# Gated delta rule beside an FP4 feed-forward layer: a loop that overlaps steps of three elements, a second buffer of values, and lanes that GpSimd turns

## The chip, the cores and the metric

One core of a Trainium2 chip runs the whole program. The metric is device time in microseconds (us): the median of the executions shown, and beside it one execution that the hardware profiler took. The engines are TensorE (PE, matrix products and transposes, out of SBUF into PSUM), VectorE (DVE), ScalarE (ACT), GpSimd (POOL) and SyncE (SP, which here only starts DMA transfers). Each has its own instruction stream, in order, and they meet at semaphores.

## What is computed

Input is x of shape (32, 256, 128): 32 independent elements of a batch, 256 steps of time, 128 channels, float32. For each element, with xn the layer norm of x:

```python
q = silu(causal_conv(xn @ Wq)); k = silu(causal_conv(xn @ Wk)); v = silu(causal_conv(xn @ Wv))
gk = -exp(A_log) * softplus(xn @ Wgk + dt_bias); beta = sigmoid(xn @ Wb + b_b)
q = l2norm(q) * 64 ** -0.5; k = l2norm(k)          # 12 heads, 64 wide; v: 12 heads, 128 wide
def step(S, (qt, kt, vt, bt, gt)):                 # 256 steps of time, S: 64 x 128 for each head
    S = S * exp(gt)
    delta = (vt - kt @ S) * bt
    S = S + outer(kt, delta)
    return S, qt @ S
o = scan(step); o = o * rsqrt(mean(o * o) + 1e-5) * g_norm_weight
attn = (o * silu(xn @ Wg)) @ Wo
ffn = fp4_linear(silu(fp4_linear(xn, w_gate)) * fp4_linear(xn, w_up), w_down)   # 352 hidden
out = x + attn + ffn
```

fp4_linear rounds both operands to an FP4 grid with one scale for each 16 numbers.

## The kernel before, in words

The scan over time is done in two chunks of 128 steps. Inside a chunk the recurrence becomes a triangular system for each head, 2 x 12 = 24 units for an element. `UP` holds for each unit the 128x128 triangle and the decayed products of queries and keys. The triangle is inverted in three stages. First its four diagonal 32x32 blocks are inverted on POOL: the blocks of all units are brought by DMA to one partition each (96 "lanes", tile `laneA`), where each lane is solved column by column with two instructions a column, 30 columns in all (`LANEP`). The columns grow from 30 numbers to 240 and shrink again. `LOUT` writes the blocks to DRAM (4 transfers), `LLOAD` reads them as lanes, `STORE` writes the solved lanes, `FETCH` puts them back into `UP` (4 transfers). Then PE joins 32-blocks to 64-blocks (`MY`, `MZ`) and those to 128 (`MY2`, `MX`, `MZ2`). For `MY` one operand must be turned: `MT` on DVE transposes solved blocks 0 to 2 of `UP` into `N64` (three instructions for each third of the units).

One element is cut into some 200 named steps, and the table `ORDER` at the head of the file is the program: each engine walks it and issues its own part of each step, in that order. A step is (kind, number, offset): in iteration `it` it works on element `it + offset`. With offset 1 stands the front of the next element: `LN`, `LN2` (layer norm), `XN` (transpose on PE), `ZB` (gates; `ZBr`, `ZBe`, `ZBg` read them), `QK`, `QKr`, `QKt`, `QKs` (keys and queries: product on PE, first tap on ACT, three taps of the convolution on DVE, silu on ACT), `QT`, `QN` (squares and their sums), `CJ` (scales), `DDg`, `DD` (decays: POOL, PE, ACT), `GR`, `GRr` (products of keys, scaled into `UP` by DVE), `VP`, `VPt`, `VPs` (values), `XQ`, `FU`, `HQ`, `HT` (feed-forward), `VT` (values turned into `V`), `KT`, and three of the four `LANEP` pieces. With offset 0 stands the back of the current element: the last piece, `STORE`, `FETCH`, `MT` to `MZ2`, then the recurrence in slots 3 to 18 (`SE` on PE and ACT, `SO` on PE and DVE, `SQ` squares on ACT), `OS` (POOL takes a power -0.5), `GP` (output gates), `OG` (DVE multiplies), `OT`, `WO` (output product), `YO`, `YOr`. The 12 heads pass through the slots as through a pipe, one head a slot.

Six PSUM banks (`ring`) are handed out along the table by `ring_plan`. Keys, queries, `UP` and several small tiles exist twice, taken by the parity of the element (`par()`); `V` exists once, so that `VT` of the next element waits for `OT` of the current one. Iterations -1 and 0 are written out, then a hardware loop runs two iterations a round, then the last is written out. In the profile L873 to L876 are `LN`, L880 `LN2` (its power -0.5 is POOL L538), L885 `ZBr`, L899 a part of `ZBg`, L856 the taps, L950 `GRr`, L1005, L1007 and L1011 `SO`, L1016 the DVE part of `OS` and L577 its POOL part, L1027 `OG`, L1034 `YOr`, L986 `MT`, L563, L568 and L571 `LANEP`, L549 `DDg`, L1098 `XN`, L1324 `WO`.

The lines that join layer norm to POOL's queue, and the turning that DVE does:

```python
if kind == "LN":                     # GpSimd
    pool.wait_ge(s_var, cnt(i, 1, 1))
    nc.gpsimd.tensor_tensor(out=rstd[:, :], in0=veps[:, :], in1=mhalf[:, 0:NT],
                            op=ALU.pow).then_inc(s_rstd, 1)
```

Of the kernel before, what the change touches and what calls it, by code (L numbers as in the profile page):

```python
# [23 lines left out]
PIECES = 4  # L24
# [27 lines left out]
    ("VT", 2, 0), ("LN", 0, 1), ("LN2", 0, 1), ("VT", 5, 0), ("VTr", 2, 0), ("XN", 0, 1), ("XNr", 0, 1),  # L52
    ("QK", 0, 1), ("ZB", 0, 1), ("ZBr", 0, 1), ("QK", 1, 1), ("QKr", 0, 1), ("ZBe", 0, 1), ("QK", 2, 1),
    ("QKt", 0, 1), ("QKr", 1, 1), ("ZBg", 0, 1), ("LANEP", 3, 0), ("DDg", 0, 1), ("STORE", 0, 0), ("QKs", 0, 1),
    ("QK", 3, 1), ("VT", 4, 0), ("QKr", 2, 1), ("VP", 0, 1), ("QKt", 1, 1), ("QKs", 1, 1), ("QKt", 2, 1),
    ("QKr", 3, 1), ("VTr", 5, 0), ("VTr", 4, 0), ("DD", 0, 1), ("FETCH", 0, 0), ("VPr", 0, 1), ("QKs", 2, 1),
    ("QT", 0, 1), ("QTr", 0, 1), ("QKt", 3, 1), ("MT", 0, 0), ("QN", 0, 1), ("QT", 1, 1), ("QTr", 1, 1),
    ("MT", 1, 0), ("QT", 2, 1), ("DDg", 1, 1), ("DD", 1, 1), ("QTr", 2, 1), ("QKs", 3, 1), ("DDr", 0, 1),
    ("GC", 0, 1), ("MY", 0, 0), ("DDg", 2, 1), ("MYr", 0, 0), ("XQ0", 0, 1), ("QN", 1, 1), ("VP", 1, 1),
    ("GCr", 0, 1), ("QK", 4, 1), ("MZ", 0, 0), ("DDr", 1, 1), ("DD", 2, 1), ("QKr", 4, 1), ("MZr", 0, 0),  # L60
    ("DDg", 3, 1), ("DDr", 2, 1), ("MY2", 0, 0), ("MY", 1, 0), ("QKt", 4, 1), ("QT", 3, 1), ("VP", 2, 1),
    ("MYr", 1, 0), ("VPr", 1, 1), ("MY2r", 0, 0), ("VPr", 2, 1), ("QTr", 3, 1), ("MZ", 1, 0), ("MT", 2, 0),
    ("SSr", 0, 1), ("MY", 2, 0), ("MZr", 1, 0), ("DD", 3, 1), ("MYr", 2, 0), ("DDr", 3, 1), ("QN", 2, 1),
    ("MX", 1, 0), ("MZ2r", 0, 0), ("CJ", 0, 1), ("QK", 5, 1), ("SE", 3, 0), ("VPt", 1, 1), ("MY2r", 1, 0),
    ("QKs", 4, 1), ("MZ", 2, 0), ("GR", 0, 1), ("VPt", 2, 1), ("VPt", 0, 1), ("GRr", 0, 1), ("GRr", 1, 1),
    ("QKr", 5, 1), ("DDg", 4, 1), ("SE", 4, 0), ("MZr", 2, 0), ("GR", 1, 1), ("QKt", 5, 1), ("XQ0", 1, 1),
# [1287 lines left out]
```

## Time and profile before

| what | value |
|---|---|
| median of 3 executions | 3294.02 us (3276.98 to 3296.87) |
| profiled execution, own time | 3276.51 us |
| its span from first to last instruction | 3274.8 us |
| busy, share of the span | PE 83%, PEld 65%, DVE 80%, ACT 67%, POOL 47% |
| mean granted clock of PE | 0.937 |
| DMA engines, mean busy share | 0.1 (22 GB/s) |

Busy time is the union of an engine's instructions. No engine is busy all the time, so the question for each stretch is which wait ends last there. The profiled execution lies 17.5 us under the median; sums below are made against its span of 3274.8 us.

### The profile page before, as it was taken

To read this page: it belongs to the slowest core of one execution; us is meant where nothing else is said; L and a number is where in the kernel's file an instruction comes from. 1 tells how busy PE (TensorE), PEld (TensorE's weight loads), DVE (VectorE), ACT (ScalarE), POOL (GpSimd) and SP (SyncE) were. 2 spreads that over 40 slices of the span, in tenths; PEclk is the share of its full clock that TensorE was granted. 3 is DMA by queue.
4 is the path that set the end of the run, shared out by engine and by line. 5 is a ranking of instruction groups with operands and counts; after the bars stand their busy time and mean duration, and the time that the engine had idled before them with its cause. 6 is when DMAs were issued, how large, how long until landed. Compare 5 with 4: busy or idle time off the path is not lost.

```text
span 3274.8 us, 84555 instructions
## 1 busy us (share of the span) xinstructions
PE 2721.0 (83%) x25330; PEld 2140.6 (65%) x25487; DVE 2617.8 (80%) x7460; ACT 2193.7 (67%) x6594; POOL 1549.4 (47%) x2386
## 2 busy tenths in 40 slices
...
GB/s 48 22 25 18 20 27 14 27 26 17 23 26 16 26 22 17 26 18 23 26 20 19 27 15 26 26 17 23 26 16 26 26 16 23 27 15 27 26 15 14
DMA packets 241563, 73.30 MB, mean 22 GB/s; under 512 B 207408, under 2 KB 234352, under 8 KB 241008
## 3 DMA queue, kind: packets, MB, share of 16 engines
...
## 4 chain that ended last, share of the span: by engine, by line
DVE 33%; POOL 27%; issue 23%; DMA 6%; PE 6%; SPq 2%; POOLq 1%; DVEq 1%; ACT 1%; ACTq 0%
POOL laneA L571 12%; POOL laneT L568 12%; DVE KQ L856 8%; DVE UP L950 8%; DVE vc L856 4%; DVE N L986 3%; DMA laneA<-to_lanes 3%; DMA to_lanes<-UP 3%; PE ring L1127 2%; POOL rO L577 2%; SPq L473 1%; POOLq L533 1%; DVE ssr L919 1%; DVE xn L880 1%; DVE V L1005 1%
## 5 line engine op out<-in xcount | busy, mean ns | idle before, releaser
L571 POOL TENSOR_TENSOR laneA<-laneA,laneT 96x30 f32<-96x30 f32 (+14 forms) x960 | 514.7, 536 | 75.6
L568 POOL TENSOR_TENSOR laneT<-laneA 96x30 f32<-96x30 f32 (+14 forms) x960 | 488.4, 509 | 68.1 <-POOL laneA L571 0.2
L555 POOL TENSOR_TENSOR sqk<-sse,phalf 128x8 f32<-128x8 f32 x96 | 157.3, 1638 | 700.5 <-DVE sse L924 700.5
L856 DVE SCALAR_TENSOR_TENSOR KQ<-ring,ckq,KQ 128x255 f32<-128x255 f32 (+2 forms) x1152 | 462.9, 475 | 14.4 <-DVE nabs L888 7.0
L856 DVE SCALAR_TENSOR_TENSOR vc<-ring,cvv,vc 128x255 f32<-128x255 f32 (+2 forms) x1152 | 460.0, 475 | 1.2
L549 POOL TENSOR_TENSOR gm<-g,mle 128x512 f32<-128x512 f32 x192 | 197.2, 1048 | 361.8 <-DVE UP L950 270.1
L577 POOL TENSOR_TENSOR rO<-ov,mhalf 128x8 f32<-128x8 f32 x96 | 162.2, 1690 | 357.6 <-DVE ov L1016 350.4
L950 DVE SCALAR_TENSOR_TENSOR UP<-ring,cj,gm 128x256 f32<-128x256 f32 x768 | 317.2, 478 | 2.3 <-PE ring L1144 1.2
L1027 DVE SCALAR_TENSOR_TENSOR V<-V,rO,ring 128x128 f32<-128x128 f32 x768 | 214.8, 343 | 121.5 <-POOL rO L577 62.3
L758 ACT ACTIVATE junk<-V 128x128 f32<-128x128 f32 x768 | 233.8, 314 | 107.0 <-DVE V L1011 96.9
L1127 PE MATMUL ring<-xnT,wqk 128*128 128x256 f32 x768 | 268.3, 501 | 16.8 <-ACT xnT L623 15.2
L1118 PE MATMUL ring<-gm,mgt 128*128 128x512 f32 x384 | 216.7, 647 | 69.5 <-POOL gm L549 55.4
L1291 PE MATMUL bank_o<-Sb,KQ 128*128 128x128 f32 x1536 | 244.7, 282 | 2.9 <-ACT V L732 1.2
L1005 DVE SCALAR_TENSOR_TENSOR V<-bank_o,negG,V 128x128 f32<-128x128 f32 x384 | 133.6, 348 | 123.6 <-PE bank_o L1297 91.3
L1127 PEld LDWEIGHTS ring<-xnT,wqk 128*128 128x128 f32 x768 | 185.2, 255 | 64.4 <-ACT xnT L623 25.9
L1158 PE MATMUL ring<-xnT,wv 128*128 128x256 f32 x768 | 210.9, 397 | 17.0 <-DVE V L1027 10.4
L1291 PEld LDWEIGHTS bank_o<-Sb,KQ 128*128 128x128 f32 x1536 | 202.7, 192 | 30.2 <-issue 11.6
L642 ACT ACTIVATE KQ<-ring,ckq 128x256 f32<-128x256 f32 x384 | 159.3, 465 | 88.9 <-PE ring L1127 88.1
L1144 PE MATMUL ring<-KQ 64*128 64x256 f32 x768 | 198.9, 393 | 22.4 <-issue 13.7
L1145 PE MATMUL ring<-KQ 64*128 64x256 f32 x768 | 199.9, 394 | 0.0
L749 ACT ACTIVATE otb<-ring 128x512 f32<-128x512 f32 x192 | 116.2, 605 | 123.3 <-PE ring L1305 83.5
L1324 PE MATMUL ring<-wo,otb 128*128 128x128 f32 x1536 | 196.6, 277 | 0.0
(164 smaller groups left out, 7703.8 us busy)
## 6 DMA issues: line engine op xcount, KB each, us to landing
to_lanes<-UP SPq DMA_DIRECT2D x128, 96.0 KB, 2.2
...
UP<-from_lanes SPq DMA_DIRECT2D x128, 96.0 KB, 2.4
...
```

Source lines behind the costliest of these rows:

```text
L568: link(nc.gpsimd.tensor_tensor(t, A[:, 0:m, j:j + 1].broadcast_to([LANES, m, n]), A[:, j:j + 1, j + 1:BLK].broadcast_to([LANES, m, n]), AL ...
L571: link(nc.gpsimd.tensor_tensor(w, w, t, ALU.add))
L577: nc.gpsimd.tensor_tensor(out=rO[:, :, uq], in0=ov[:, :, uq], in1=mhalf[:, 0:8].rearrange("p (t h) -> p t h", t=NT), op=ALU.pow).then_inc( ...
L758: ins = nc.scalar.activation(junk[:, t, :], V[:, t, h, :], ACT.Square, accum_out=ssO[:, t, h:h + 1])
L856: ins = nc.vector.scalar_tensor_tensor(acc[:, n, s:T], src[:, n * T:n * T + T - s], wt(n)[:, TAPS - 1 - s:TAPS - s], acc[:, n, s:T], ALU.m ...
L950: ins = nc.vector.scalar_tensor_tensor(UP[:, par(), NT * a + t, :, :], b[:, t * 2 * P:(t + 1) * 2 * P].rearrange("p (k n) -> p k n", k=2), ...
L1027: ins = nc.vector.scalar_tensor_tensor(v, v, rO[:, t, 4 * q + n:4 * q + n + 1], gate[:, n * P:(n + 1) * P], ALU.mult, ALU.mult)
L1118: mm(b[:, :], mgt[:, :], decay(a).rearrange("p h t n -> p (h t n)"), start=True, stop=False)
L1127: ins = mm(b[:, w * T:(w + 1) * T], wqk[:, w, a * P:(a + 1) * P], xnT[:, par(), :], start=True, stop=True)
L1145: o_done = mm(odd[:, o], KQ[krows(1), a, 0, ts], KQ[krows(1), a, :, ts], start=True, stop=True)
L1158: ins = mm(b[:, n * T:(n + 1) * T], wv[:, h * P:(h + 1) * P], xnT[:, par(), :], start=True, stop=True)
L1291: ins = mm(BO[:, w * P:(w + 1) * P], KQ[:, h // 2, w, P:2 * P], Sb[:, h % 2, :], start=True, stop=True)
```

## The change

`ORDER` is a new table. Its offsets now run from 0 to 2: `LN` and `LN2` stand at offset 2, in the middle of an iteration, so that in iteration `it` the layer norm of element `it + 2` is taken. The lane solve has `PIECES` = 8 pieces of up to four columns, of which 0 to 5 stand at offset 1 and 6, 7 at offset 0. `MT` is gone: after the last piece POOL copies 72 of the 96 lanes, rows and columns exchanged, into a new tile `laneX`; `TSTORE` writes it to DRAM and `TFETCH` brings it with three transfers into `N64`, which now has room for all units. `V` becomes `V2`, taken by parity, and `VT` waits for `OT` of two elements before. `sq` has two buffers for four. The exponent of `GC` is taken by two ACT instructions, straight into `eG2`, and a DVE copy goes. Six iterations are written out ahead of the loop and two behind it, so the loop has 13 rounds for 15. Semaphore counts follow the three offsets.

```diff
-PIECES = 4
+PIECES = 8
+TURNED = 3
...
+        V2 = sb("V2", [P, 2, NT, NH, P])
+        laneX = sb("laneX", [P, BLK, BLK])
-        sq = sb("sq", [P, 4, 2 * NT * 2, DK])
+        sq = sb("sq", [P, 2, 2 * NT * 2, DK])
-        N64 = sb("N64", [P, 2, GU, 2, BLK])
+        N64 = sb("N64", [P, NU, 2, BLK])
...
-            for it in (-1, 0):
+            for it in range(-2, 4):
...
-            with eng.Fori(1, NB - 2, 2) as it:
+            with eng.Fori(4, NB - 3, 2) as it:
...
+                    if kind == "TSTORE":
+                        sp.wait_ge(s_turn, cnt(i, 1, 1))
...
+                        sp.dma_start(turned.rearrange("q u j i -> (q u) (j i)"),
+                                     laneX[0:TURNED * NU, :, :].rearrange("l j i -> l (j i)")).then_inc(s_tout, 16)
+                    if kind == "TFETCH":
+                        sp.wait_ge(s_tout, cnt(i, 1, 1) * 16)
...
+                        for q in range(TURNED):
+                            r = slice(BLK * q, BLK * q + BLK)
+                            sp.dma_start(N64[r, :, q % 2, :], turned[q].rearrange("u j i -> j u i")).then_inc(s_xcd, 16)
...
                         if a == PIECES - 1:
                             pool.sem_inc(s_solved, 1)
+                            if not zero(i):
+                                pool.wait_ge(s_tout, i * 16)
+                                hold(pool)
+                            nc.gpsimd.tensor_copy(laneX[0:TURNED * NU, :, :],
+                                                  laneA[0:TURNED * NU, :, :].rearrange("l j i -> l i j")).then_inc(s_turn, 1)
...
                     if kind == "QT":
-                        if a >= 4 or not zero(i):
-
-                            act.wait_ge(s_sums, cnt(i, NP, a - 3) if a >= 4 else cnt(i - 1, NP, a + 3))
+                        if a >= 2 or not zero(i):
+
+                            act.wait_ge(s_sums, cnt(i, NP, a - 1) if a >= 2 else cnt(i - 1, NP, a + 5))
...
-                    if kind == "MT":
-
-                        if a == 0:
-                            dve.wait_ge(s_xc, cnt(i, 1, 1) * 16 * NBL)
...
-                            ins = nc.vector.transpose(corner(a)[r, :, q % 2, :], UP[r, par(), units(a), 0, r])
...
                     if kind == "MY":
                         b = take("MY", a)
-                        pe.wait_ge(s_xcd, cnt(i, NG, a + 1))
+                        if a == 0:
+                            pe.wait_ge(s_xcd, cnt(i, 1, 1) * 16 * TURNED)
...
+                        if a == 0:
+                            pe.wait_ge(s_xc, cnt(i, 1, 1) * 16 * NBL)
```

**DVE, end of an iteration and start of the next.** `V<-V,rO,ring` is `OG`, `vc` and `KQ` are taps, `yb` is `YOr`, `z` is `ZBr`, `stats` and `mv` are layer norm. Before:

```order
281 L960 TENSOR_TENSOR Kt<-ring,kr 128x384
282 L1027 SCALAR_TENSOR_TENSOR V<-V,rO,ring 128x128 x4
283 L856 SCALAR_TENSOR_TENSOR vc<-ring,cvv,vc 128x255 x2
284 L856 SCALAR_TENSOR_TENSOR vc<-ring,cvv,vc 128x254 x2
285 L856 SCALAR_TENSOR_TENSOR vc<-ring,cvv,vc 128x253 x2
286 L1034 COPY yb<-ring 128x256
287 L802 TENSOR_TENSOR hs<-qv,qs 128x704
288 L941 TENSOR_TENSOR V<-ring,sqk 128x512
289 L960 TENSOR_TENSOR Kt<-ring,kr 128x384
290 L359 UNCONDITIONAL_BRANCH
291 L359 ISA
292 L873 BN_STATS stats<-xin 128x6
293 L846 ISA
294 L875 BN_AGGR mv<-stats 128x2
```

The changed kernel, written-out iterations 1 and 2:

```order
577 L1071 SCALAR_TENSOR_TENSOR V<-V,rO,ring 128x128 x8
578 L995 TENSOR_TENSOR V<-ring,sqk 128x512 x2
579 L854 TENSOR_TENSOR hs<-qv,qs 128x704
580 L1071 SCALAR_TENSOR_TENSOR V<-V,rO,ring 128x128 x8
581 L911 SCALAR_TENSOR_TENSOR vc<-ring,cvv,vc 128x255 x2
582 L911 SCALAR_TENSOR_TENSOR vc<-ring,cvv,vc 128x254 x2
583 L911 SCALAR_TENSOR_TENSOR vc<-ring,cvv,vc 128x253 x2
584 L1078 COPY yb<-ring 128x256
585 L940 TENSOR_TENSOR z<-ring,zbias 128x48
586 L943 TENSOR_SCALAR nabs<-z 128x24
587 L911 SCALAR_TENSOR_TENSOR KQ<-ring,ckq,KQ 128x255 x2
588 L911 SCALAR_TENSOR_TENSOR KQ<-ring,ckq,KQ 128x254 x2
```

What stood between `yb` and `z` (a feed-forward product, values, keys, layer norm) is gone from there: the `z` of the next element follows `yb` directly, and layer norm stands earlier, among the `GRr`.

**POOL, end of the lane solve.** `laneA` and `laneT` are the last columns, `gm` is `DDg`. Before, with layer norm's power (`rstd`) ahead of the last seven columns (two of them shown apart):

```order
73 L568 TENSOR_TENSOR laneT<-laneA 96x184
74 L571 TENSOR_TENSOR laneA<-laneA,laneT 96x23x8
75 L538 TENSOR_TENSOR rstd<-veps,mhalf 128x2
76 L568 TENSOR_TENSOR laneT<-laneA 96x168
77 L571 TENSOR_TENSOR laneA<-laneA,laneT 96x24x7
```

Here the last column is followed by the `DDg`. The changed kernel:

```order
158 L611 TENSOR_TENSOR laneA<-laneA,laneT 96x29x2
159 L608 TENSOR_TENSOR laneT<-laneA 96x30
160 L611 TENSOR_TENSOR laneA<-laneA,laneT 96x30
161 L617 COPY laneX<-laneA 72x1024
162 L589 TENSOR_TENSOR gm<-g,mle 128x512 x4
163 L595 TENSOR_TENSOR sqk<-sse,phalf 128x2x4
164 L589 TENSOR_TENSOR gm<-g,mle 128x512
165 L595 TENSOR_TENSOR sqk<-sse,phalf 128x2x4
166 L578 TENSOR_TENSOR rstd<-veps,mhalf 128x2
167 L589 TENSOR_TENSOR gm<-g,mle 128x512
168 L595 TENSOR_TENSOR sqk<-sse,phalf 128x2x4
```

The power for layer norm left the lane solve and stands between the third and fourth `DDg` groups; the turning copy stands between the last column and the first `DDg`.

**SP, the transfers of one iteration.** `xin` is `LN`, `laneX` and `turned_lanes` are `TSTORE` and `TFETCH`, `N` is `N64`. Before:

```order
23 L456 DMA xin<-in_L_attn_hidden_states_dram 128x2x128
24 L487 DMA from_lanes<-laneA 96x1024
25 L493 DMA UP<-from_lanes 32x24x32 x4
26 L473 DMA to_lanes<-UP 32x24x32 x4
27 L460 DMA xres<-in_L_attn_hidden_states_dram 128x2x128
28 L479 DMA laneA<-to_lanes 96x1024
29 L463 DMA out_dram<-yb 128x2x128
```

The changed kernel:

```order
32 L515 DMA turned_lanes<-laneX 72x1024
33 L507 DMA from_lanes<-laneA 96x1024
34 L525 DMA N<-turned_lanes 32x24x32 x3
35 L530 DMA UP<-from_lanes 32x24x32 x4
36 L475 DMA xin<-in_L_attn_hidden_states_dram 128x2x128
37 L492 DMA to_lanes<-UP 32x24x32 x4
38 L499 DMA laneA<-to_lanes 96x1024
39 L479 DMA xres<-in_L_attn_hidden_states_dram 128x2x128
40 L482 DMA out_dram<-yb 128x2x128
```

Four transfers are new; `FETCH` (`UP<-from_lanes`) stands behind the three of `TFETCH`.

## Rows read from the trace of the kernel before

**Rows 1.** The page: busy time of each engine, and the chain that ended last.

```profile
PE 2721.0 (83%) x25330; PEld 2140.6 (65%) x25487; DVE 2617.8 (80%) x7460; ACT 2193.7 (67%) x6594; POOL 1549.4 (47%) x2386
...
DVE 33%; POOL 27%; issue 23%; DMA 6%; PE 6%; SPq 2%; POOLq 1%; DVEq 1%; ACT 1%; ACTq 0%
```

**Rows 2.** Timeline of VectorE (DVE), one iteration: start us, length us, instruction.

```profile
1517.07 0.21 DVE L885 TENSOR_TENSOR z<-ring,zbias 128x48 f32<-128x48 f32 x1 [2.81 <-PE ring L1106]
...
1564.24 3.23 DVE L950 SCALAR_TENSOR_TENSOR UP<-ring,cj,gm 128x256 f32<-128x256 f32 x8
...
1598.64 1.13 DVE L1027 SCALAR_TENSOR_TENSOR V<-V,rO,ring 128x128 f32<-128x128 f32 x4 [4.29 <-POOL rO L577]
...
1611.29 0.29 DVE L873 BATCH_NORM_STATS2 stats<-xin 128x6 f32<-128x128 f32 x1 [3.00 <-issue]
...
1618.81 0.21 DVE L885 TENSOR_TENSOR z<-ring,zbias 128x48 f32<-128x48 f32 x1 [4.01 <-PE ring L1106]
```

**Rows 3.** Timeline of GpSimd (POOL): lane solve and what stands with it.

```profile
1576.46 0.50 POOL L563 MEMSET laneA<- 96x32 f32 x1 [3.17 <-DMA laneA<-to_lanes]
...
1596.96 1.64 POOL L577 TENSOR_TENSOR rO<-ov,mhalf 128x8 f32<-128x8 f32 x1
...
1612.95 0.70 POOL L538 TENSOR_TENSOR rstd<-veps,mhalf 128x2 f32<-128x2 f32 x1 [3.02 <-DVE veps L876]
...
1619.82 0.26 POOL L571 TENSOR_TENSOR laneA<-laneA,laneT 96x30 f32<-96x30 f32 x1
...
1676.19 0.15 POOL L563 MEMSET laneA<- 96x32 f32 x1 [1.15 <-DMA laneA<-to_lanes]
```

**Rows 4.** Timeline of the DMA queue (SPq): LOUT in two iterations.

```profile
1567.56 2.10 SPq L473 DMA_DIRECT2D to_lanes<-UP  x4
...
1669.31 2.10 SPq L473 DMA_DIRECT2D to_lanes<-UP  x4
```

**Rows 5.** Timeline of TensorE (PE): XN.

```profile
1514.32 0.44 PE L1098 MATMUL ring<-ident,xn 128*128 128x128 f32 x2 [2.78 <-DVE xn L880]
```

**Rows 6.** Windows: us, busy PE, PEld, DVE, ACT, POOL; clock, DMA, GB/s.

```profile
1613.00:1711.00 98.00, 85.29 (x797) 66.78 (x800) 81.23 (x233) 69.46 (x210) 49.29 (x76) 0.95 0.10 22
```

**Rows 7.** Groups by line: busy us, mean ns of one.

```profile
L1027 DVE SCALAR_TENSOR_TENSOR V<-V,rO,ring 128x128 f32<-128x128 f32 x768 | 214.8, 343 | 121.5 <-POOL rO L577 62.3 <-ACT ring L670 59.3
...
L986 DVE STREAM_TRANSPOSE N<-UP 32x256 f32<-32x256 f32 x288 | 124.1, 431 | 21.5 <-DMA UP<-from_lanes 14.0 <-PE ring L1082 4.9
...
L941 DVE TENSOR_TENSOR V<-ring,sqk 128x512 f32<-128x512 f32 x96 | 65.9, 686 | 0.7 <-PE ring L1166 0.7
...
L802 DVE TENSOR_TENSOR hs<-qv,qs 128x704 f32<-128x704 f32 (+1 forms) x33 | 29.1, 883 | 7.6 <-DVE yb L1034 7.5
...
L506 POOL MEMSET N<- 128x1024 f32 x1 | 1.0, 951 | 0.0
```

**Rows 8.** Timelines of DVE and POOL, elements 1, 2 and 31.

```profile
124.77 1.11 DVE L880 TENSOR_SCALAR xn<-xin,mv,rstd 128x128 f32<-128x128 f32 x2 [17.89 <-POOL rstd L538]
130.02 0.21 DVE L885 TENSOR_TENSOR z<-ring,zbias 128x48 f32<-128x48 f32 x1 [4.13 <-PE ring L1106]
...
133.59 1.07 DVE L899 TENSOR_SCALAR eb<-eb 128x24 f32<-128x24 f32 x1
...
135.03 4.76 DVE L856 SCALAR_TENSOR_TENSOR KQ<-ring,ckq,KQ 128x255 f32<-128x255 f32 x12
...
133.57 4.06 POOL L549 TENSOR_TENSOR gm<-g,mle 128x512 f32<-128x512 f32 x4 [2.43 <-DVEq L897]
...
227.41 0.21 DVE L885 TENSOR_TENSOR z<-ring,zbias 128x48 f32<-128x48 f32 x1 [4.01 <-PE ring L1106]
...
3100.77 0.21 DVE L885 TENSOR_TENSOR z<-ring,zbias 128x48 f32<-128x48 f32 x1 [4.01 <-PE ring L1106]
```

**Rows 9.** Timelines of POOL and DVE, last iteration.

```profile
3199.58 0.26 POOL L571 TENSOR_TENSOR laneA<-laneA,laneT 96x30 f32<-96x30 f32 x1
...
3206.88 2.69 DVE L986 STREAM_TRANSPOSE N<-UP 32x256 f32<-32x256 f32 x6 [13.98 <-DMA UP<-from_lanes]
```

More of the change, by code:

```diff
@@ L51 @@
 ORDER = (
[L52 to L66, printed above, removed]
[3 rows of a table removed]
@@ L87 @@
-    ("OTr", 3, 0), ("GPr", 5, 0), ("OT", 4, 0), ("WO", 2, 0), ("OG", 5, 0), ("WO", 3, 0), ("OTr", 4, 0),
-    ("OT", 5, 0), ("WO", 4, 0), ("OTr", 5, 0), ("VPt", 5, 1), ("WO", 5, 0), ("VT", 3, 1), ("YOr", 0, 0),
-    ("HQ", 3, 1), ("HT", 0, 1), ("LANEP", 2, 1), ("HTr", 0, 1), ("VPs", 5, 1), ("HT", 1, 1), ("HTr", 1, 1),
-    ("KT", 1, 1), ("VTr", 3, 1), ("KTr", 1, 1),
+    ("XN", 0, 1), ("XNr", 0, 1), ("LANEP", 6, 0), ("VPs", 4, 0), ("QK", 0, 1), ("ZB", 0, 1), ("QK", 1, 1),
+    ("ZBr", 0, 1), ("VPs", 5, 0), ("LANEP", 7, 0), ("QKr", 0, 1), ("ZBe", 0, 1), ("VT", 2, 0), ("QKt", 0, 1),
@@ new lines @@
+    ("ZBg", 0, 1), ("VT", 5, 0), ("QKr", 1, 1), ("QK", 2, 1), ("VTr", 2, 0), ("GC", 0, 1), ("QKr", 2, 1),
+    ("TSTORE", 0, 0), ("QKt", 1, 1), ("VT", 4, 0), ("VP", 0, 1), ("QK", 3, 1), ("VTr", 5, 0), ("GCr", 0, 1),
+    ("QKs", 0, 1), ("QKt", 2, 1), ("QKs", 1, 1), ("VP", 1, 1), ("DDg", 0, 1), ("DDg", 1, 1), ("QT", 0, 1),
+    ("VPr", 0, 1), ("QKr", 3, 1), ("QTr", 0, 1), ("DDg", 2, 1), ("QT", 1, 1), ("QKs", 2, 1), ("DDg", 3, 1),
+    ("VTr", 4, 0), ("VP", 2, 1), ("QKt", 3, 1), ("QK", 4, 1), ("QTr", 1, 1), ("VPr", 1, 1), ("QKs", 3, 1),
@@ new lines @@
+    ("STORE", 0, 0), ("QT", 2, 1), ("DD", 0, 1), ("QTr", 2, 1), ("TFETCH", 0, 0), ("DD", 1, 1), ("QKr", 4, 1),
+    ("QN", 0, 1), ("VPt", 1, 1), ("DDr", 0, 1), ("DD", 2, 1), ("DDr", 1, 1), ("QKt", 4, 1), ("VPr", 2, 1),
+    ("DDr", 2, 1), ("DD", 3, 1), ("FETCH", 0, 0), ("DDr", 3, 1), ("MY", 0, 0), ("MYr", 0, 0), ("MY", 1, 0),
+    ("QN", 1, 1), ("MY", 2, 0), ("VPt", 2, 1), ("MZ", 0, 0), ("MYr", 1, 0), ("QT", 3, 1), ("VPt", 0, 1),
+    ("MZr", 0, 0), ("QK", 5, 1), ("MZ", 1, 0), ("MY2", 0, 0), ("SSr", 0, 1), ("XQ0", 0, 1), ("CJ", 0, 1),
@@ new lines @@
+    ("MYr", 2, 0), ("GR", 0, 1), ("MZr", 1, 0), ("MY2r", 0, 0), ("QKr", 5, 1), ("MX", 1, 0), ("QTr", 3, 1),
+    ("QKt", 5, 1), ("VPs", 0, 1), ("QKs", 4, 1), ("GRr", 0, 1), ("QN", 2, 1), ("MZ", 2, 0), ("XQ0", 1, 1),
+    ("MZ2r", 0, 0), ("SE", 3, 0), ("QKs", 5, 1), ("QN", 3, 1), ("GRr", 1, 1), ("MY2r", 1, 0), ("QT", 4, 1),
+    ("SE", 4, 0), ("MZr", 2, 0), ("DDg", 4, 1), ("GR", 1, 1), ("GRr", 2, 1), ("GR", 2, 1), ("QT", 5, 1),
+    ("QTr", 4, 1), ("SE", 5, 0), ("QN", 4, 1), ("GRr", 3, 1), ("QTr", 5, 1), ("SSr", 1, 1), ("SO", 5, 0),
[4 rows of a table added]
@@ L91 @@
+    ("DDr", 5, 1), ("SO", 8, 0), ("XQr", 0, 1), ("VPs", 2, 1), ("GR", 5, 1), ("GRr", 10, 1), ("SE", 9, 0),
[15 rows of a table added]
+    ("HTr", 0, 1), ("OT", 4, 0), ("WO", 3, 0), ("OG", 5, 0), ("HTr", 1, 1), ("LANEP", 5, 1), ("OTr", 4, 0),
+    ("OT", 5, 0), ("WO", 4, 0), ("OTr", 5, 0), ("WO", 5, 0), ("VPt", 5, 1), ("YOr", 0, 0),
 )
@@ L526, in iteration @@
                 i0, base = (0, 0) if first_it else (it, chain[2])
-                if not first_it:
+                if isinstance(it, int) and it == NB - 1:
+                    i0, base = 0, 0
+                    chain[1] = chain[0] + (NB - 2) * chain[2] + chain[3]
+                elif not first_it:
                     chain[1] = chain[0]
```

128 lines of the change are left out of this document (73 added, 55 removed), and 34 rows, old and new, of the table ORDER.

## The prediction

> **What bounds the kernel now.** I read the page first. DVE is busy for 80% of the span and PE for 83%, so neither is the limit by itself; the chain that ended last names DVE for 33% and POOL for 27%, although POOL is busy for only 47% [rows 1]. So I followed one iteration on DVE, POOL and the queue. From z (ZBr, 1517.07) to the end of the last GRr (1564.24 + 3.23 = 1567.47) DVE works almost without a gap: 50.4 us [rows 2]. LOUT is issued at that moment (1567.56) [rows 4], the lanes are in at 1576.46, and POOL solves them, with the OS powers among them, until it reaches layer norm's power at 1612.95 [rows 3]. Behind that power stand xn, XN on PE, and the next z at 1618.81, for which DVE waits 4.01 us [rows 2]. This is a ring: front of an element, LOUT, 24 of 30 columns on POOL, layer norm of the next element, its front. It takes (3100.77 - 227.41) / 29 = 99.1 us an iteration [rows 8], against 81.2 us of DVE and 85.3 us of PE work in 98 [rows 6]. Layer norm is a few us of work which stands in POOL's queue behind a solve that it does not need. The first round shows this barest: DVE waits 17.89 us for the power [rows 8].
>
> **The change, part by part.** All times from z to z, in the middle of the run.
>
> Layer norm at offset 2 takes POOL's power out of the ring. DVE's LN and LN2 work (about 1.4 and 1.0 us) remains, only elsewhere. What is late next? I walk round the new order. (1) z to the last GRr: 50.4 us, less nine transposes of 0.431 us (3.9) [rows 7], less a copy of 0.1, plus LN's 1.4, which now stands among the GRr: 47.8. (2) LOUT and LLOAD to the first column: 1567.56 to 1576.46 is 8.9 us, 1669.31 to 1676.19 is 6.9 [rows 3, 4]: 7.9. (3) Pieces 0 to 3, the first 15 columns: 1576.46 to 1596.96 is 20.5, of which one OS power (1.64) is now ahead of the solve: 18.9. (4) OS 1, which stands behind piece 3 in POOL's queue: 1596.96 to the OG that waited for such a power, 1598.64: 1.7 [rows 2, 3]. (5) DVE's tail: OG 2 to 5 are 16 instructions, four in 1.12 us with the next one 1.03 us behind (4.2), two VTr (0.69 each) and HQ 3 (0.88) [rows 2, 7]: 6.4. (6) OT 5, its copy by ACT, WO 5: 1.7, an estimate: two groups on PE at the 0.44 that XN's pair takes [rows 5], and a copy as long as both. (7) XN follows WO 5 at once, since xn is long ready: 1514.32 to 1517.07, 2.75 us [rows 2, 5]. The sum is 47.8 + 7.9 + 18.9 + 1.7 + 6.4 + 1.7 + 2.75 = 87.2 us. VPt 5 and YOr fill DVE while PE does (6).
>
> At the edge of the loop every engine stands still (3.00 us of "issue") [rows 2], every second iteration. Some is hidden by POOL's chain; I add 1.2: 88.4. That is the floor of this ring. What it lacks: PE. Its 85.3 us of work [rows 6] would fill 93% of 91.5 us. The old iteration left PE 12.7 us idle, of which the 2.78 for xn go [rows 5]. If all the rest stays, PE gives 95 us; if waits overlap, as they do where two engines are near full, less. I take the middle, 91.5, a gain of 7.6 us, and keep 88.4 and 95 as ends. A steadier PE also sees its fast clock for longer (the granted clock of the window is 0.95 [rows 6]), which speaks for the lower half; strict order on five engines speaks for the upper.
>
> The lane solve from the other side. POOL now has OS 1 and OS 2 together ahead of piece 4, so LANEP 4 to 7, the copy and all DDg stand behind a wait for the last output square. OS 2 ends at 47.8 + 28.5 + 1.6 = 77.9 after z; the other 15 columns take 17.8 us (1598.6 to 1620.1 without layer norm's power and the idle time ahead of it) [rows 3], to 95.7, that is 4.2 us into the next iteration. The turning copy has no row. 1024 numbers a lane: the POOL memset of 128x1024 takes 0.951 us [rows 7]; the solve's own instructions of 240 numbers start 0.7 us apart (15 columns, 30 instructions, in 18.9 us, with shorter ones among them), which scaled to 1024 gives 2.8. Its read is strided, as the solve's is in part, so I take 2.0, with 1.0 and 2.8 as ends. DDg then starts 6.2 us after z, against 133.57 - 130.02 = 3.6 before [rows 8]; the table meets this by having DD 0 on PE behind QT 2. TSTORE and TFETCH are four transfers. In the last iteration store and fetch took 3199.84 to 3206.88, 7.0 us [rows 9]; the new pair is as long, FETCH is issued behind it, about 1.5 us later. MY 0 can start 13.2 us after z, MZ 0 some 2 us later, behind three more products of PE than before. Slack here is small, one or two us, and I price it at nothing on top of the 91.5.
>
> Second V: VT no longer waits for OT. VT's waits before were short, and it only frees the planner; nothing. Two sq buffers: QTr 2 must wait for QN 0, ACT is busy for 67% and its queue behind that instruction holds DDr 0 and QKr 4, needed 2 us later; nothing, 1 us at worst. GC: one more ACT instruction, 0.2 us, covered. More code written out: no row shows a stall away from loop edges; two edges fewer give back some 5 us, within the rounding.
>
> A rule against this change: POOL's copy beside DVE. The row: DVE's eb, usually near 0.2 us, took 1.07 at 133.59 while the first DDg ran on POOL from 133.57, yet 12 taps (135.03, 4.76 us) beside the other DDg kept their 0.39 each [rows 8]. So small SBUF-only instructions lose up to one POOL instruction, taps nothing. The copy falls beside ZBg and the taps behind it; ZBg is ahead of GC and DDg. By this I expect up to 1 us an iteration, held in the 91.5. The Trainium skill, "SBUF — State Buffer", section "SBUF: two separate sides", says that GpSimd and certain DVE instructions share one pair of ports, as a lock held for a whole instruction. By that rule the price would be as long as the copy whenever both meet, some 60 us over the run in place of 30; the row of eb agrees with the lock, that of the taps shows who escapes it.
>
> **The run.** Middle: 29 x 7.6 = -220. Start: z of element 1 was at 130.02, after 17.89 us of waiting [rows 8]; that wait goes, so 112.1. But element 0's lanes end no earlier (133.57 less 2.43 us of idle time is 131.1) [rows 8], and the copy and the transfers follow, so that DDg and MY of iteration 0 come some 15 us late: z of element 2 at 112.1 + 91.5 + 15 = 218.6, in place of 227.41: -9. End: the last back starts some 4 us earlier and pays 2 for the copy and the later fetch: -2. 3274.8 - 231 = 3044 for the span, 3045.5 for its execution. The profiled execution before lies 17.5 us under the median; with the same added, 3063, say 3060 us.
>
> **Rivals.** (a) PE is the bound: its waits stay, with those of the recurrence's slots added where DVE had slack before. 95 to 98 us an iteration: 3150 to 3245. For it: 85.3 of 98 busy. Against: part of PE's idle time is the very stretch that goes.
> (b) The ring closes at its floor, 88.4 or a little under: 2970 or less.
> (c) The gain goes into new waits and nothing is measured: 98.1 to 100.3 us an iteration, 3261 to 3327. It needs both (a) and the wait of POOL's queue.
> (d) Slower: the turned lanes. Everything between the last column and MY 0 is serial: copy, store, fetch. With one or two us of slack each further us goes into the period, since MZ 0 stands ahead of GR 0 on PE and GR feeds the GRr that LOUT waits for. It decides from about 7.6 + 2 = 10 us more than my 9: a strided copy of 12 us or more, that is above 11 ns a number against 2.7 in the solve. At 16 us the period is 104 and the time 3420. Against: the solve reads with strides too.
> (e) POOL's copy holds DVE up for its whole length every time: 1 us more an iteration, 3090, inside the forecast's range.
>
> **Chances.** Floor or under (below 2990): 0.08. Forecast (2990 to 3150, 89.2 to 94.6 us): 0.56. (a): 0.21. (c): 0.07. (d) and other mishaps, slower by over 1%: 0.08. Faster by over 1%, which is about what a measurement of this kernel can tell from no change: 0.85; within 1%: 0.07; slower: 0.08. For 8 in 10 I take the forecast whole and most of (a), and a little of (b): 2985 to 3220.
>
> **What would show it.** Right: z to z near 91 us; DVE's wait for z under 3 us and none for the power at layer norm; OG 2 waits for POOL's power (step 4); no STREAM_TRANSPOSE; POOL's copy near 2 us, beginning 4 us after z. Wrong: PE over 92% busy with z to z at 95 (a); PE waiting at MY 0 or MZ 0 for a transfer, or at DD 0 for POOL (d).

## The result

| | before | after |
|---|---|---|
| median, us | 3285.82 (3276.98 to 3296.87) | 3198.43 (3193.51 to 3204.98) |
| profiled execution, us | 3276.51, span 3274.8 | 3198.38, span 3196.7 |
| z to z, mean of elements 3 (before), 4 (after) to 31, us | 99.16 | 97.15 |

The median before is now one of four executions. The ratio is 0.973, 95% interval 0.969 to 0.978: 87 us less, where 226 were forecast. The page of the changed kernel, busy time and chain (they answer to [rows 1]):

```profile
PE 2694.1 (84%) x25423; PEld 2119.8 (66%) x25487; DVE 2514.9 (79%) x7140; ACT 2189.9 (69%) x6626; POOL 1646.4 (52%) x2418
...
POOL 24%; issue 24%; DVE 19%; PE 18%; DMA 7%; ACT 4%; SPq 2%; POOLq 1%; DVEq 1%; ACTq 0%
```

DVE has lost the transposes (2618 to 2515 us busy), POOL has gained the copy, the rest is as it was. The page doesn't show what went wrong. The distance from z to z does. Timeline of DVE in the changed kernel, `z` and `yb` alone (they answer to [rows 2]; the first three rows are from an iteration that is written out ahead of the loop, the others from the loop):

```profile
402.13 0.21 DVE L940 TENSOR_TENSOR z<-ring,zbias 128x48 f32<-128x48 f32 x1 [1.82 <-PE ring L1152]
...
490.85 0.43 DVE L1078 COPY yb<-ring 128x256 f32<-128x256 f32 x1 [1.13 <-PE ring L1373]
493.02 0.21 DVE L940 TENSOR_TENSOR z<-ring,zbias 128x48 f32<-128x48 f32 x1 [1.75 <-PE ring L1152]
...
1650.72 0.42 DVE L1078 COPY yb<-ring 128x256 f32<-128x256 f32 x1 [1.83 <-PE ring L1373]
1660.88 0.21 DVE L940 TENSOR_TENSOR z<-ring,zbias 128x48 f32<-128x48 f32 x1 [9.73 <-PE ring L1152]
...
1755.66 0.21 DVE L940 TENSOR_TENSOR z<-ring,zbias 128x48 f32<-128x48 f32 x1 [1.75 <-PE ring L1152]
...
1855.24 0.21 DVE L940 TENSOR_TENSOR z<-ring,zbias 128x48 f32<-128x48 f32 x1 [9.70 <-PE ring L1152]
```

Written out, an iteration takes 493.02 - 402.13 = 90.9 us. In the loop the two of a round take 94.8 and 99.6 here. In what follows an "edge" is the place at which the loop turns back: the jump from the last instruction of its body to the first, which every engine makes for itself. Behind each of the 12 edges, and only there, DVE waits some 9 us for z (8.9 to 9.7) in place of 1.8. What it waits for, on PE at that place:

```profile
1648.60 2.09 PE L1373 MATMUL ring<-wo,otb 128*128 128x128 f32 x16
1656.92 0.69 PE L1144 MATMUL ring<-ident,xn 128*128 128x128 f32 x2 [6.24 <-issue]
1658.09 2.07 PE L1173 MATMUL ring<-xnT,wqk 128*128 128x256 f32 x4 [0.47 <-ACT xnT L673]
1659.95 0.89 PE L1152 MATMUL ring<-wzb,xnT 128*128 128x24 f32 x4
```

The last WO of one element is done at 1650.69, and XN of the next, which waits for nobody, begins 6.24 us later; "issue" says that the trace shows no releaser. The 12 such pauses last 5.4 to 6.2 us. Written out, XN follows at once. The pause costs more than its length. Windows of the changed kernel (us, busy PE, PEld, DVE, ACT, POOL, then the granted clock of PE as a share of full speed):

```profile
402.10:493.00 90.90, 80.03 (x795) 63.11 (x797) 77.49 (x222) 68.07 (x208) 51.42 (x76) 1.00 0.14 30
...
1660.90:1755.70 94.80, 85.41 (x795) 67.05 (x798) 77.22 (x223) 67.97 (x208) 47.28 (x65) 0.94 0.14 29
```

```profile
1650.00:1655.00 5.00, 0.69 (x7) 0.49 (x5) 0.42 (x1) 0.00 (x0) 1.79 (x4) 1.00 0.14 38
1655.00:1660.00 5.00, 2.60 (x7) 1.84 (x8) 0.00 (x0) 1.42 (x3) 4.21 (x10) 0.55 0.02 7
1660.00:1665.00 5.00, 4.71 (x25) 3.91 (x24) 3.50 (x12) 4.22 (x12) 3.50 (x7) 0.77 0.04 13
...
1685.00:1690.00 5.00, 3.02 (x89) 2.38 (x88) 4.70 (x17) 4.95 (x9) 0.60 (x1) 0.96 0.01 2
1690.00:1695.00 5.00, 4.70 (x22) 4.08 (x24) 3.30 (x9) 3.66 (x10) 1.05 (x1) 0.50 0.01 3
```

The windows of 0.55 and 0.77 say that from late in the pause on PE has the lower of its two levels (1.2 GHz, 0.5 of full speed) for some 7 us, just where XN, QK and ZB stand between DVE and its z; the two transposes of xn take 0.69 us there and 0.38 in the iteration that is written out. It falls there again at 1690, behind a thinner stretch. The same 795 products cost 85.4 us in this iteration and 80.0 at a clock of 1.00. Not all of that is the edge's doing: with no edge at all (e1 below) they cost between 79.9 and 85.4 us an iteration, 82.3 on average, at clocks of 1.00 down to 0.93.

### The profile page after: what moved, and what is told of

It reads as the page before. It is cut to its first block, busy times and chain, and to the rows that moved or that the text cites. A ratio compares the mean times of both kernels' runs of the same rounds, so it can differ in the third digit from the quotient of the medians.

```text
span 3196.7 us, 83151 instructions
## 1 busy us (share of the span) xinstructions
PE 2694.1 (84%) x25423; PEld 2119.8 (66%) x25487; DVE 2514.9 (79%) x7140; ACT 2189.9 (69%) x6626; POOL 1646.4 (52%) x2418
## 3 DMA queue, kind: packets, MB, share of 16 engines
q14 instruction: 297, 2.43, 0.3%
## 4 chain that ended last, share of the span: by engine, by line
POOL 24%; issue 24%; DVE 19%; PE 18%; DMA 7%; ACT 4%; SPq 2%; POOLq 1%; DVEq 1%; ACTq 0%
POOL laneA L611 10%; POOL laneT L608 9%; DVE KQ L911 5%; DVE vc L911 4%; DMA laneA<-to_lanes 4%; PE ring L1373 4%; DMA to_lanes<-UP 3%; PE ring L1173 3%; DVE UP L1004 2%; POOL gm L589 2%; PE ring L1204 2%; POOL rO L622 2%; DVE V L1071 2%; POOL sqk L595 2%; PE ring L1190 1%
## 5 line engine op out<-in xcount | busy, mean ns | idle before, releaser
L611 POOL TENSOR_TENSOR laneA<-laneA,laneT 96x30 f32<-96x30 f32 (+14 forms) x960 | 541.9, 564 | 75.2
L608 POOL TENSOR_TENSOR laneT<-laneA 96x30 f32<-96x30 f32 (+14 forms) x960 | 497.5, 518 | 110.7 <-issue 38.4
L1004 DVE SCALAR_TENSOR_TENSOR UP<-ring,cj,gm 128x256 f32<-128x256 f32 x768 | 325.8, 477 | 51.1 <-PE ring L1190 36.5
L773 ACT ACTIVATE eps<-bank_e 128x128 f32<-128x128 f32 x384 | 106.2, 277 | 304.3 <-PE bank_e L1326 212.1
L1173 PE MATMUL ring<-xnT,wqk 128*128 128x256 f32 x768 | 238.9, 439 | 73.8 <-DVE KQ L911 48.5
L1309 PE MATMUL bank_e<-V,UP 128*128 128x128 f32 x768 | 179.1, 317 | 78.1 <-ACT UP L766 68.0
L1190 PE MATMUL ring<-KQ 64*128 64x256 f32 x768 | 233.3, 443 | 4.3 <-DVE UP L1004 2.6
L1191 PE MATMUL ring<-KQ 64*128 64x256 f32 x768 | 233.4, 443 | 0.0
L1173 PEld LDWEIGHTS ring<-xnT,wqk 128*128 128x128 f32 x768 | 147.2, 213 | 123.5 <-DVE KQ L911 61.2
L1164 PE MATMUL ring<-gm,mgt 128*128 128x512 f32 x384 | 207.8, 623 | 24.2 <-POOL gm L589 21.3
L1219 PE MATMUL ring<-wg,xnT 128*128 128x512 f32 x384 | 210.4, 631 | 10.3 <-DVE V L1071 10.0
```

The source lines that it names most:

```text
L608: link(nc.gpsimd.tensor_tensor(t, A[:, 0:m, j:j + 1].broadcast_to([LANES, m, n]), A[:, j:j + 1, j + 1:BLK].broadcast_to([LANES, m, n]), AL ...
L611: link(nc.gpsimd.tensor_tensor(w, w, t, ALU.add))
L1004: ins = nc.vector.scalar_tensor_tensor(UP[:, par(), NT * a + t, :, :], b[:, t * 2 * P:(t + 1) * 2 * P].rearrange("p (k n) -> p k n", k=2), ...
L1173: ins = mm(b[:, w * T:(w + 1) * T], wqk[:, w, a * P:(a + 1) * P], xnT[:, par(), :], start=True, stop=True)
L1190: e_done = mm(even[:, o], KQ[krows(0), a, 0, ts], KQ[krows(0), a, :, ts], start=True, stop=True)
L1191: o_done = mm(odd[:, o], KQ[krows(1), a, 0, ts], KQ[krows(1), a, :, ts], start=True, stop=True)
```

## The experiments

Each time is the median of its executions on the chip. The kernel before gave 3283.3, 3279.6 and 3281.5 in the three groups (e1 to e4, e5 to e8, e9 to e12), so some 4 us of a difference across groups mean nothing. "Ratio" is against the kernel before in the same group, with its 95% interval.

**e1: no loop.** The loop of the changed kernel written out.

```diff
-            for it in range(-2, 4):
+            for it in range(-2, NB):
                 parity[0] = it % 2
                 iteration(it)
-            with eng.Fori(4, NB - 3, 2) as it:
...
```

> The changed kernel with its loop written out: the same steps in the same order, but no iteration is run by a hardware loop, so that there is no back edge. Theory 'edge': the 12 back edges are the whole of what is missing. The iterations that are written out in the changed kernel took 90.9 to 92.5 us from z to z, the 25 that the loop reaches took 97.6 on average (585.33 to 3025.28). Without the edges all take 91.0 to 92.5: 3198 - 25 x 6.0 = 3048, between 3030 and 3070. Theory 'pauses only': just the pauses of 7.5 us go and the other loop iterations stay at 95.5: 3198 - 12 x 7.5 = 3108. Theory 'it wears in' (transfers, turned lanes or PE's clock limit the middle of the run at 96 to 99 us, whatever the loop): 3180 to 3200.

Measured: 3067.8 us, ratio 0.933 (0.929 to 0.936). z to z is 92.2 us on average (402.94 to 2893.15, 27 iterations) and the wait for z 1.82 from element 2 on. "Edge" holds, at the upper end of its range. Single iterations take 90.5 to 95.6 us, and the middle of the run is no slower than its start.

**e2: the kernel before, without its loop.** The same edit of the old one, `range(-1, NB)`.

> The kernel before with its loop written out, as e1. Theory 'edge': in the old order an edge cost DVE 3.0 us of issue and the mean over the pair 1.2 us an iteration, so 14 edges give 3286 - 14 x 2.4 = 3252, at most 3286 - 14 x 5 = 3216 if the lower granted clock behind the edge goes as well. Rival: the edge costs the old order as much as the new one (7 to 12 us each): 3286 - 14 x 10 = 3146, and then the new order has no more than 100 us over it without edges either.

Measured: 3231.6 us, ratio 0.984 (0.981 to 0.987); z to z 97.5. The 14 edges of the old order cost 52 us, 3.7 each, between the two theories and near the first. Without any edge the change is worth 3231.6 - 3067.8 = 164 us (5%).

**e3: half as many edges.** Four iterations in a round of the loop.

```diff
-            for it in range(-2, 4):
+            for it in range(-2, 6):
...
-            with eng.Fori(4, NB - 3, 2) as it:
-                for n in range(2):
+            with eng.Fori(6, NB - 5, 4) as it:
+                for n in range(4):
```

> The changed kernel with four iterations in the body of the loop in place of two: 5 back edges in place of 12. Theory 'edge': each edge carries 150/12 = 12.5 us with what follows it, so 3198 - 7 x 12.5 = 3110 (3095 to 3125). Theory 'it wears in': 3180 to 3200. If a longer body makes an edge dearer, 3125 to 3198.

Measured: 3095.0 us, at the low end of the range. An edge costs (3095.0 - 3067.8) / 5 = 5.4 us here against (3198.4 - 3067.8) / 12 = 10.9 in the changed kernel. The trace had a second thing to show: at the same step, XN behind the last WO, PE's pause was 2.8 to 3.2 us at the five edges, and not 5.4 to 6.2.

**e4: the edge elsewhere.** The same cyclic order, cut at another step; PSUM buffers are given out by the uncut table, since at the new place some are in use.

```diff
+EDGE = 34
...
 def steps_of_an_iteration():
-    return list(ORDER)
+    return list(ORDER[EDGE:]) + [(kind, a, off + 1) for kind, a, off in ORDER[:EDGE]]
...
```

> The changed kernel with the same order and the same loop of two iterations, but the place at which the loop turns back is moved by 34 steps, from in front of XN to in front of the first QT, where DVE has several taps queued and PE waits for them. Theory 'place' (an edge is dear because the new order puts XN, QK and z right behind it, with nothing queued on DVE): the pause of PE is covered in part by DVE's queue, an edge costs 3 to 5 us less than 12.5, 3198 - 12 x 4 = 3150 (3135 to 3170). Theory 'PE pays anywhere' (PE is busy for 85 of 91 us, so its 6.2 us pause and the lower clock behind it cost the same wherever they fall): 3185 to 3210.

Measured: 3095.6 us, 103 less than the changed kernel, twice what "place" gave it. It had changed two things at once: the place, and the pause, which was 31.5 / 12 = 2.6 us. So the length of the pause had to be separated from the place of the edge.

**e5 and e6: PE's code shifted, nothing else.** 16 (e6: 128) increments of a semaphore that nobody waits for, ahead of PE's first iteration.

```diff
+            for _ in range(16):
+                hold(pe)
             run(pe, iteration)
```

> The changed kernel with 16 more semaphore instructions in PE's program ahead of its first iteration, and nothing else: every later instruction of PE lies 16 places further on. PE's pause behind an edge was 6.2 us in the changed kernel (the loop's body starts at instruction 7118 of PE's program), 2.8 us in e3 at the same step of the order (it starts at 10456) and 2.5 to 3.2 us in e4 (7217). Theory 'where the code lies': a pause of 6.2 us is two of about 3 in a row, because the body's first instructions straddle two blocks that are brought one after the other; 7118 is 206 beyond a multiple of 256 and 10456 is 216, so a shift by 16 ends it: pause 2.8 us, and the edge costs what it did in e3, (93.15 - 92.23) x 27 / 5 = 5.0 us in place of 11: 3068 + 12 x 5 = 3128 (3105 to 3150). Theory 'the steps at the edge': the pause belongs to XN behind the last WO in a body of two iterations, and the shift changes nothing: 3190 to 3205. The Trainium skill, page 'Runtime: NRT & Kernel Launch', section 'Instruction fetch mechanics', says that instructions come in blocks of 16 KiB (256 instructions) and that a taken branch out of the blocks at hand stalls until its target has been fetched; by it the first theory holds if a second block is wanted too.

> The same with 128 instructions in place of 16 (the body starts at 7245, 77 beyond a multiple of 256). 'Where the code lies': as e5, pause 2.8 us and about 3128 us. 'The steps at the edge': 6.2 us and 3190 to 3205.

Measured: 3124.5 us (ratio 0.954, 0.951 to 0.957) and 3142.2 us (0.958, 0.955 to 0.961; two executions). e6's z of element 0 comes at 46.5 us in place of 36.4, so without its later start it is at 3132; from z of element 5 to that of element 31 the two take the same, 2455.6 and 2456.7 us, where the changed kernel takes 2532.3. Sixteen instructions that do nothing made the kernel 74 us faster. Waits of PE for "issue" at XN, of the changed kernel and of e5 (total us, times, longest):

```profile
PE ring L1144 <- issue: 70.4, 12, 6.2
```

```profile
PE ring L1144 <- issue: 36.8, 13, 3.1
```

5.9 us a turn have become 2.9 (the first of e5's 13, 2.46 us at 25.48, is not an edge); in e6 it is 2.9 too. The clock changes with the pause: the two transposes of xn behind the edge take 0.69 us at all 12 edges of the changed kernel, but 0.43 at 9 of e5's and 11 of e6's. So the long pause costs its 3 us more and the lower clock behind it. The place, XN, is the same, and so is the number of edges: an edge costs (3124.5 - 3067.8) / 12 = 4.7 us.

**e7: the mild place with the long pause.** e4 with 158 of these instructions.

> e4 (the edge in front of QT 0, 3095.6 us, pause 2.5 to 3.2) with 158 instructions more ahead of PE's first iteration, so that the body starts at 7375 in place of 7217: the same 206 beyond a multiple of 256 as in the changed kernel. 'Where the code lies': the pause becomes 6 us there as well. If the place in the order counts beside it, the longer pause is partly under DVE's queue: 3095.6 + 12 x 2 = 3120 (3105 to 3135); if only the length of the pause counts, 3190. 'The steps at the edge': 3095 and pauses of 2.5 to 3.2.

Measured: 3161.9 us (0.963, 0.961 to 0.966). Waits of PE at the edge in e4 and in e7:

```profile
PE ring L1191 <- issue: 31.5, 12, 3.2
```

```profile
PE ring L1191 <- issue: 72.9, 12, 6.9
```

The long pause can be made at will, at another step of the order. It costs more there than expected: z of element 0 is 14.4 us later than in e4, and the other 52 us are 4.3 for each edge, against 6.2 at XN. That split is rough: at z of element 6, ahead of the first edge, e7 is only 5.4 us behind e4, and from there to z of element 31 it takes 59.5 us longer, 5.0 for each edge. At equal pauses QT is the better place by 2.4 us (short) and some 4 us (long) an edge. The four corners:

| edge at | short pause | long pause |
|---|---|---|
| XN | 3124.5 (e5) | 3198.4 (changed kernel) |
| QT 0 | 3095.6 (e4) | 3147.5 (e7 less its 14.4) |

Counted in the compiled program, loop bodies that started 49, 59, 77, 216 or 221 instructions beyond a multiple of 256 of PE's program (e4, e12, e6, e3, e5) had the short pause, both that started 206 beyond it (the changed kernel, e7) the long one. That instructions come in blocks and that the long pause is two of them fetched in a row fits this, and fits the Trainium skill, "Runtime: NRT & Kernel Launch", "Instruction fetch mechanics" (blocks of 256, and a stall at a taken branch whose target isn't at hand). The page has no case of two blocks, and no run here shows a fetch; what the runs show is that the pause hangs on where the code lies. Why 206 is long and 216 short stays open.

**e8: DVE turns again.** e1 with the turning copy, `TSTORE` and `TFETCH` taken out and `MT` put back (after FETCH, MY 0 and MY 1).

> The loop written out (e1, 3067.8 us) with one part of the change undone: DVE turns the inverses again (nine transposes an iteration, 431 ns each in the profile before = 3.9 us) behind the fetch of the solved lanes, and the copy on POOL with its four transfers is gone. Prediction's reading: DVE is on the path from z to z, so 31 x 3.9 = +121, less what DVE idles there: 3068 + 60 to 120 = 3130 to 3190. Rival 'PE is the bound' (its busy time is 87% of e1's span and the rest are waits of its own): +0 to +30 us, 3068 to 3098. Rival 'turned lanes hurt' (their transfers stand before FETCH in SP's queue): below 3060.

Measured: 3176.8 us (0.968, 0.966 to 0.970), 109 more than e1: 3.5 us an iteration for 3.9 us of transposes. Two thirds of the 164 us of e2 to e1 come from this part; new order, layer norm, pieces and second `V` have 3231.6 - 3176.8 = 55 between them. That it is DVE's own work that is paid is not shown, since the transposes also stand between FETCH and MY. PE's waits at MY, e1 and e8 ("issue" here: the trace names no releaser):

```profile
PE ring L1243 <- issue: 17.3, 1, 17.3
```

```profile
PE ring L1247 <- issue: 90.8, 96, 17.7
```

By the two timelines MZ 0 starts 19.8 us after z in e1 and 22.3 in e8 (means of elements 8 to 29), 2.5 us later. In e10 below DVE has no more work than in e1, MZ 0 starts 2.1 us later, and 2.4 us an iteration are paid. So the later lanes can account for most of the 3.5, and e8 shows the price of the whole exchange only.

**e9: would the kernel before have suffered?** Its PE code shifted by 145.

> The kernel before, its loop untouched, with 145 more semaphore instructions in PE's program ahead of its first iteration. Its loop's body starts at instruction 2110 (62 beyond a multiple of 256), PE's pauses behind an edge are 4.6 to 4.9 us; now it starts at 2255, 207 beyond. Theory 'where the code lies' (not a property of the new order): the pause grows by some 3 us there too, and 14 edges of 3 to 6 us more and a start that is up to 11 us later (e6: z for the first time at 46.5 in place of 36.4) give 3280 + 42 to 95 = 3322 to 3375. Rival 'only the new order is open to it': 3280 to 3295.

Measured: 3281.7 us, ratio 1.000 (0.998 to 1.001). PE's waits at its edge, of the kernel before and of e9:

```profile
PE ring L1166 <- issue: 64.0, 14, 4.9
```

```profile
PE ring L1166 <- issue: 85.9, 14, 6.6
```

The pause grew here too, from 4.6 to 6.1 us, and nothing came of it: z of element 31 is at 3105.28 in place of 3100.77, though that of element 0 came 11 us later. The rival holds. In the old order XN stands behind LN, POOL's power and LN2 of the same element, all after the edge. In the kernel before PE still waits 0.5 to 1.2 us for xn (2.2 once) when its pause is over, so that much of a longer pause is free. In e9 that wait is gone and XN begins 0.4 to 1.5 us after xn is ready; why this rest does not show either (the iterations with an edge take 101.2 us in place of 101.6) stays open. And the pause was only 1.5 us longer here, not 3, so the test is half as hard as it was meant to be. In the new order xn lies ready since the middle of the iteration before, and XN meets the pause bare.

**e10: two copies.** e1 with the turning copy done twice.

```diff
+                            link(nc.gpsimd.tensor_copy(laneX[0:TURNED * NU, :, :],
+                                                       laneA[0:TURNED * NU, :, :].rearrange("l j i -> l i j")))
```

> The loop written out (e1, 3067.8) with the copy that turns the lanes on POOL done twice, each 2.0 us, one behind the other: every transfer of solved lanes starts 2.1 us later. The prediction put the slack between the lanes' end and MY, which wants them, at 1 to 2 us and priced the copy at nothing. By it: 31 x (2.1 - 1.5) = +19, 3075 to 3100. Rival 'no slack': 31 x 2.1 = +65, 3125 to 3140. Rival 'lanes have slack of over 2 us': 3060 to 3075.

Measured: 3142.4 us (0.956, 0.952 to 0.960), 74.6 more than e1, 2.4 us an iteration for 2.07 us of copy. There is no slack at all. The second copy also makes DDg start 2.0 us later on POOL, but PE's wait for `gm` grows only from 21.0 to 24.2 us over the whole run. The lanes are what is missed: MY 0 starts 0.7 us and MZ 0 2.1 us later after z than in e1. PE's waits for the fetched lanes at MZ, e1 and e10:

```profile
PE ring L1255 <- DMA UP<-from_lanes: 5.5, 10, 1.4
```

```profile
PE ring L1257 <- DMA UP<-from_lanes: 43.2, 31, 2.5
```

**e11: four pieces.** e1 with `PIECES = 4`.

```diff
-    ("XN", 0, 1), ("XNr", 0, 1), ("LANEP", 6, 0), ("VPs", 4, 0), ("QK", 0, 1), ("ZB", 0, 1), ("QK", 1, 1),
-    ("ZBr", 0, 1), ("VPs", 5, 0), ("LANEP", 7, 0), ("QKr", 0, 1), ("ZBe", 0, 1), ("VT", 2, 0), ("QKt", 0, 1),
+    ("XN", 0, 1), ("XNr", 0, 1), ("VPs", 4, 0), ("QK", 0, 1), ("ZB", 0, 1), ("QK", 1, 1),
+    ("ZBr", 0, 1), ("VPs", 5, 0), ("LANEP", 3, 0), ("QKr", 0, 1), ("ZBe", 0, 1), ("VT", 2, 0), ("QKt", 0, 1),
...
```

> The loop written out (e1, 3067.8) with the lane solve in four pieces in place of eight, each pair of pieces at the place of its second half (the first half of each so starts later, behind steps that POOL had between them). Prediction's reading: the small pieces let POOL's other steps slip in without holding the lanes or being held; 31 x 1 to 3 us = 3095 to 3160. Rival 'the number of pieces doesn't matter': 3060 to 3075.

Measured: 3054.4 us (0.930, 0.926 to 0.933), 13 less than e1, just outside the rival's range and far from mine. Eight pieces bring nothing, with all steps at these places; why four are a little quicker stays open (the last column ends 0.1 us earlier after z than in e1, the last GRr 0.5). This is the fastest version here.

**e12: e3 and e4 together.**

> Both mild forms together: the edge in front of QT 0 (e4) and a body of four iterations (e3), 5 edges in place of 12; the body starts at 10555, 59 beyond a multiple of 256. An edge at QT with a short pause cost (3095.6 - 3067.8) / 12 = 2.3 us: 3068 + 5 x 2.3 = 3080 (3070 to 3090). If its edges cost what those of e3 did, 5 us: 3093.

Measured: 3087.9 us, in the range. By this sum an edge costs (3087.9 - 3067.8) / 5 = 4.0 us in place of 2.3. Over five edges that is 8 us, and the executions of e1 alone spread over 10: not told apart.

## Why the prediction missed

The step that failed is the **edge of the loop**: "every second iteration. Some is hidden by POOL's chain; I add 1.2". It measured (3198.4 - 3067.8) / 29 = 4.5 us an iteration, 3.3 more than it was given. The middle came out at 96.8 us from z to z (below), 5.3 over the 91.5; the other 2.0 lie in the ring itself. The runs share the 130.6 us out: 28 are what 12 edges cost at best (e4), 29 are their place in front of XN (e5 less e4), 74 are the long pause (changed kernel less e5). The working took DVE's 3.00 us [rows 2] for the pause of every engine, though the rows show DVE's alone, and left it where it was. But PE's own pause was longer already, and under cover. The kernel before at the edge of [rows 2], PE:

```profile
1607.11 0.49 PE L1152 MATMUL ring<-ident,KQ 128*128 128x128 f32 x3
1612.25 1.96 PE L1166 MATMUL ring<-ident,vc 128*128 128x128 f32 x8 [4.65 <-issue]
1614.86 0.69 PE L1098 MATMUL ring<-ident,xn 128*128 128x128 f32 x2 [0.65 <-DVE xn L880]
```

Taking layer norm out of the ring, rightly read as the gain, also took away what hid this: XN waited for xn, and xn was late anyway. That could be seen in advance, by asking what stands first behind the edge in the new table. The other half, that the new code would lie where the pause is 3 us longer, could not be read from a trace. That part of the miss is bad luck: with the code of PE 16 instructions further on, 74 of the 130.6 us are not there.

**z to z, 91.5 us.** 90.9 in the iteration above, 92.2 on average in e1. Walking round it as the prediction did (402.13 to 493.02), rows of the changed kernel:

```profile
409.79 2.02 POOL L617 COPY laneX<-laneA 72x1024 f32<-72x1024 f32 x1 [0.27 <-POOL laneA L611]
411.77 4.07 POOL L589 TENSOR_TENSOR gm<-g,mle 128x512 f32<-128x512 f32 x4
...
459.76 0.15 POOL L603 MEMSET laneA<- 96x32 f32 x1 [2.28 <-DMA laneA<-to_lanes]
...
479.31 3.25 POOL L622 TENSOR_TENSOR rO<-ov,mhalf 128x8 f32<-128x8 f32 x2
```

```profile
449.31 1.66 DVE L1004 SCALAR_TENSOR_TENSOR UP<-ring,cj,gm 128x256 f32<-128x256 f32 x4 [0.19 <-PE ring L1190]
...
480.99 2.15 DVE L1071 SCALAR_TENSOR_TENSOR V<-V,rO,ring 128x128 f32<-128x128 f32 x8 [1.45 <-POOL rO L622]
...
485.23 2.14 DVE L1071 SCALAR_TENSOR_TENSOR V<-V,rO,ring 128x128 f32<-128x128 f32 x8
```

Step 1: 450.97 - 402.13 = 48.8 (47.8 forecast). Steps 2 and 3: to 459.76, 8.8 (7.9), and to 479.31, 19.6 (18.9). Step 4: 1.7 (1.7). Step 5: to 487.37, 6.4 (6.4). Steps 6 and 7: 5.7 (4.45). Together 90.9 for 87.2: each step is found where it was put, and four of the six lines are forecast 0.7 to 1.2 us too short. Without an edge the forecast is 87.2 + 3.1 for PE = 90.3, and e1 measures 92.2. So 91.5 stands near the ring's true length partly by luck: the walk is 3.7 to 5 us short, and the 3.1 added for PE fill most of that. Rival (a) names the time that came out, but not its cause: PE is 84% busy, not over 92, and e1 has the same products in 92 us. PE is not out of the game either. Of e1's iterations from element 3 on the two at a granted clock of 1.00 take 90.5 and 90.8 us, the four at 0.93 to 0.95 take 93.2 to 95.6; whether the clock makes them longer or their waits lower the clock, no run separates.

**Start and end.** z of element 1 at 114.78 (112.1 forecast), of element 2 at 218.59 (218.6); from the last z to the end 171.4 us against 174.0 before (2 less forecast). All of the miss lies between: (3025.28 - 218.59) / 29 = 96.8.

**The turned lanes.** The copy takes 2.0 us as forecast. It begins 7.7 us after z, not 4, and MY 0 18.0 after z (420.08), not 13.2. DDg starts 9.6 us after z, not 6.2. Pricing this at nothing was wrong: by e10 every microsecond ahead of MZ is paid. It did not show in the sum, since step 1 had nearly the length that it was given. Rival (d) had the slope right, "each further us goes into the period", and the copy would have had to be six times as long.

**Rival (e), POOL's copy beside DVE.** It isn't so for the taps. In the changed kernel's DVE timeline beside the copy of 1661.87 to 1663.87:

```profile
1661.67 2.43 DVE L911 SCALAR_TENSOR_TENSOR KQ<-ring,ckq,KQ 128x255 f32<-128x255 f32 x6 [0.25 <-DVE nabs L943]
```

Six taps in 2.43 us are as quick as six anywhere else. The Trainium skill ("SBUF — State Buffer", "SBUF: two separate sides") puts the lock on VectorE instructions in a 2-port mode or with two SBUF inputs. A tap reads one of its two tensors from PSUM (`ring`), so the lock as stated there does not cover it, and the trace agrees: it loses nothing, like the taps of [rows 8].

**Priced at nothing.** The second `V` and the two `sq` buffers were not tried alone, so what they cost or bring is not known. The two fewer edges' "5 us" are 7, at 3.7 each in the old order.
